# Blank gather slots of a graph kernel: one shared row of lowest values, or one row for each partition

## The reference

```python
def _L0_gnn_ref(X, adj):
    neg = jnp.finfo(X.dtype).min
    mask = adj != 0
    vals = jnp.max(jnp.where(mrows[:, :, None], X[None, :, :], neg), axis=1)
    has_nbr = jnp.any(mrows, axis=1)
    return jnp.where(has_nbr[:, None], vals, 0)
...
x = _layernorm(x + _L0_gnn_ref(x, adj), axis=-1)
x = _layernorm(x + _L1_gnn_ref(x, L1_gnn_W, L1_gnn_a, adj, 8192), axis=-1)
x = _layernorm(x + _L2_gnn_ref(adj, x, L2_gnn_W, L2_gnn_a), axis=-1)
x = _layernorm(x + _L3_gnn_ref(x, adj, L3_gnn_W, L3_gnn_a), axis=-1)
```

## Time and profile before

| what | value |
|---|---|
| median of 3 runs | 5,798.88 us |
| span of the profiled execution | 6,308.7 us |
| PE, DVE, ACT, POOL busy | 84%, 76%, 32%, 18% of the span |
| DMA queue q1 | 482.61 MB, 21.4% of 16 engines' span |
| DMA queue q0 | 73.21 MB, 11.5% |
| DMA queue q10 | 67.13 MB, 3.0% |
| mean granted TensorE clock | 0.922 |

### The profile page before, as it was taken

How to read it: one execution, slowest core, us unless ns; L and a number is a source line. 1 busy time by engine, 2 the same in 40 slices (tenths; PEclk the granted TensorE clock), 3 DMA queues, 4 the chain that set the end, 5 groups by cost and what they waited for, 6 DMA issues and landing times. The chain is left out here.

```text
span 6308.7 us, 93770 instructions
## 1 busy us (share of the span) xinstructions
PE 5282.6 (84%) x24260; PEld 2436.7 (39%) x24370; DVE 4783.5 (76%) x8750; ACT 2000.3 (32%) x2798; POOL 1155.2 (18%) x1367
## 2 busy tenths in 40 slices
PE   2766767666676654999999999979999998999999
PEld 1333333333333323333333333325444445444444
DVE  4676767677776664788888888887788886888887
ACT  1444444444444422555454545410000001000000
POOL 2545445444544530000000000000000000000000
PEclk8888888888888885999999999998999997999999
DMA  5777778777777722011111111001121211221210
GB/s 193 183 182 181 189 181 190 174 189 180 187 187 186 174 56 79 34 41 42 36 41 41 42 42 42 28 35 66 67 74 67 74 47 64 74 78 64 85 61 30
DMA packets 150569, 628.53 MB, mean 100 GB/s; under 512 B 30368, under 2 KB 39008, under 8 KB 92688
## 3 DMA queue, kind: packets, MB, share of 16 engines
q1 hardware_dynamic: 78464, 482.61, 21.4%
q0 software_dynamic: 34768, 73.21, 11.5%
q10 hardware_dynamic: 36864, 67.13, 3.0%
HBM read 551.49 MB, written 75.53 MB: 99 GB/s over the span
## 5 line engine op out<-in xcount | busy, mean ns | idle before, releaser
L1215 PE MATMUL bank<-w,GX 128*128 128x512 f32 x6144 | 2835.8, 607 | 31.7 <-DVE w L1442 22.6
L1215 PEld LDWEIGHTS bank<-w,GX 128*128 128x128 f32 x6144 | 1128.4, 191 | 1403.3 <-issue 1395.4
L1456 DVE SCALAR_TENSOR_TENSOR w<-q,E,m 128x512 f32<-128x512 f32 x2048 | 1449.1, 748 | 280.7 <-PE bank L1215 188.4
L283 POOL DMA_INDIRECT ring<-x_ext,idx x1051 | 1026.5, 977 | 1180.3 <-DVE X L519 354.8
L507 DVE TENSOR_TENSOR top<-top,sums 128x1024 f32<-128x1024 f32 x496 | 604.2, 1218 | 637.3 <-remote 379.1
L418 PE MATMUL sums<-lone,xs 128*128 128x512 fp8e4 x3072 | 857.7, 421 | 250.4 <-DVE top L507 136.5
L348 ACT ACTIVATE stage<-tp 128x1024 fp8e4<-128x1024 uint16 x512 | 523.5, 1024 | 1202.3 <-PE tp L390 573.4
L1442 DVE SCALAR_TENSOR_TENSOR w<-q,E,u 128x512 f32<-128x512 f32 x1024 | 762.4, 746 | 165.8 <-PE bank L1215 165.1
L1279 ACT ACTIVATE above<-bank,offset 128x512 fp8e4<-128x512 f32 x1024 | 649.1, 684 | 639.0 <-PE bank L1143 637.2
L1431 DVE SCALAR_TENSOR_TENSOR u<-theta,E,m 128x512 fp8e4<-128x512 f32 x1024 | 766.4, 750 | 95.2 <-issue 81.7
L418 PEld LDWEIGHTS sums<-lone,xs 128*128 128x128 bf16 x3072 | 300.5, 105 | 787.0 <-issue 568.6
(11 more groups left out here) (231 smaller groups left out, 3259.2 us busy)
## 6 DMA issues: line engine op xcount, KB each, us to landing
adjb<-in_adj SPq DMA_DIRECT2D x256, 1024.0 KB
m<-mask_t SPq DMA_DIRECT2D x192, 1024.0 KB, 4.9
mask_t<-stage ACTq DMA_DIRECT2D x256, 256.0 KB
ring<-x_ext,idx POOLq DMA_INDIRECT x1051
out<-X SPq DMA_DIRECT2D x16, 256.0 KB, 2.4
nhc<-nhd POOLq DMA_DIRECT2D x32, 2.0 KB, 1.7
Wn<-in_L_gnn_W SPq DMA_DIRECT2D x3, 64.0 KB
A<-in_L_gnn_a SPq DMA_DIRECT2D x6, 0.5 KB
```

The lines of the kernel that those rows point to most:

```text
L283: pool.indirect_dma_start(ring[:, s, :], None, x_ext, bass.IndirectOffsetOnAxis(ap=idx[:, k, s:s + 1], axis=0)).then_inc(done, 16)
L1215: last = nc.tensor.matmul(acc[b][:, :], GX[:, j, :], w[:, j % WR, :], start=(j == 0), stop=(j == T - 1))
L1456: nc.vector.scalar_tensor_tensor(out=w[:, j % WR, :], in0=q, scalar=E[:, j:j + 1], in1=m[:, b, j, :], op0=ALU.max, op1=ALU.mult).then_inc( ...
```

## The change

There are 128 rows of lowest values behind x instead of one. Partition p's blank slots get the number N + p. To that end `program` makes a constant `blank` of two columns, N + p and -127 - (N + p), which take the place of the two constants in L648 and L649. `top` is set on all 128 partitions, and its 128 pieces are written to `x_ext`. Nothing else is changed: the same slots are gathered, in the same order, by the same DMAs.

```diff
-            pool.dma_start(x_ext[N:N + 1, :], top[0:1, 0, 0:F]).then_inc(low_in, 16)
+            pool.dma_start(x_ext[N:N + P, :], top[:, 0, 0:F]).then_inc(low_in, 16)
...
-            nc.vector.memset(top[0:1, 0, 0:F], -BIG).then_inc(low_ready, 1)
+            nc.vector.memset(top[:, 0, 0:F], -BIG).then_inc(low_ready, 1)
...
-                    steps.do(nc.vector.scalar_tensor_tensor(out=pad[:, :], in0=base[:, :], scalar=-127.0 - N, in1=pad[:, :], op0=ALU.add, op1=ALU.mult))
-                    nc.vector.tensor_scalar(idx[:, (k + 1) % 2, :], pad[:, :], float(N), None, ALU.add).then_inc(idx_ready, 1)
+                    steps.do(nc.vector.scalar_tensor_tensor(out=pad[:, :], in0=base[:, :], scalar=blank[:, 0:1], in1=pad[:, :], op0=ALU.add, op1=ALU.mult))
+                    nc.vector.tensor_scalar(idx[:, (k + 1) % 2, :], pad[:, :], blank[:, 1:2], None, ALU.add).then_inc(idx_ready, 1)
...
-    x_ext = nc.dram_tensor("x_ext", [N + 1, F], F32, kind="Internal").ap()
+    x_ext = nc.dram_tensor("x_ext", [N + P, F], F32, kind="Internal").ap()
...
+            blank = sb0("blank", [P, 2], F32)
...
+                blank_i = c1.enter_context(nc.sbuf_tensor("blank_i", [P, 1], I32))
...
+                    s.do(nc.gpsimd.iota(blank_i[:, :], pattern=[[0, 1]], base=N, channel_multiplier=1))
                     s.do(nc.gpsimd.memset(sel[:, :, :], 0.0))
...
-                    dve.wait_ge(again, 4)
+                    dve.wait_ge(made, 16)
+                    nc.vector.tensor_copy(blank[:, 1:2], blank_i[:, :]).then_inc(again, 1)
+                    dve.wait_ge(again, 5)
+                    nc.vector.tensor_scalar(blank[:, 0:1], blank[:, 1:2], -1.0, -127.0, ALU.mult, ALU.add).then_inc(again, 1)
+                    dve.wait_ge(again, 6)
```

More of the change, by code:

```diff
@@ L146, in neighbour_max @@
 def neighbour_max(nc, x, adj, mask_t, x_ext, nm, deg, consts):
-    ident_b, ident, powers, code_no, firsts, found, due = consts
+    ident_b, ident, powers, code_no, firsts, blank, found, due = consts
     with ExitStack() as ctx:
@@ L1554, in _ @@
                     nc.vector.tensor_copy(firsts[:, :], firsts_f[:, :, :].rearrange("p w b -> p (w b)")).then_inc(again, 1)
-                    dve.wait_ge(again, 4)
-            neighbour_max(nc, x, adj, mask_t, x_ext, X, deg, (ident_b, ident, powers, code_no, firsts, has, rstd))
+                    dve.wait_ge(made, 16)
[3 more added lines that the diff above has]
+                    dve.wait_ge(again, 6)
+            neighbour_max(nc, x, adj, mask_t, x_ext, X, deg, (ident_b, ident, powers, code_no, firsts, blank, has, rstd))
             first_norm(nc, x, X, deg, has, stats)
```

## The result

The changed kernel takes 5,758.31 us, the median of 4 runs (5,751.61 to 5,773.01), against 5,804.8 for the kernel before (4 runs): ratio 0.991, 95% interval 0.989 to 0.9929, 46 us less. The profiled execution is one of the four, 5,751.61 us with a span of 5,750.0. The span of before that all rows above come from was 6,308.7. Most of that difference is not the change's, and it is not the profiler's either: the experiments show it.

The account below looks back on a forecast made before the run. The prediction took DMA occupancy to bound stage one, 26.0 us of a 26.5 us tile. A gain of 1.2 us in 64 tiles, 77 us, less 4 us of costs, gave 5,726 us from 5,799; range 5,640 to 5,825.

Parts of the forecast that it names:

- the three queues: Stage one: gathers, mask stores and adjacency loads take 11.1, 3.0 and 11.8 us of every DMA engine a tile, 26.0 together.
- the 4 us of costs: Index arithmetic and setup: 4 us added in sum, of which 3 us for the column operands in L648 and L649.
- That rival: Gathers: the change doesn't speed the packets, slow ones come from load, not one shared row; 5,803 us, chance 0.06.
- That is the ground of my forecast: Stage one, unprofiled runs: DMA needs 26.0 us of an estimated 26.5 to 28.8 us tile, so it is 90 to 98% occupied.
- DVE as the next bound: Stage one: once DMA falls to 18.5 us a tile, DVE's 24.1 us bounds it, a gain of 0 to 2.4 us.
- The half of 2.4 us: Stage one: half the possible gain taken because hand-offs never close fully, 1.2 us a tile, 77 us over 64 tiles.
- The columns: L648 and L649: a column operand replacing a constant costs 0 to 0.05 us each, 6 us at most, 3 taken.
- The issue gaps belong to profiling: Stage one: PE's issue idle, 5.1 us a tile, and the 510 us between profiled span and median come from profiling.
- The sign that the prediction gave for profiling: PE's issue idle gone in the profile and the median moving far less than the span would show gaps from profiling.
- That they aren't from the slow packets: Stage one, against the rival that PE's issue gaps are real and come from slow packets: 325 us, 5,474, chance 0.11.
- Nothing waits for DMA: Stage one: DMA at 98% may still meet every deadline, so only the 4 us of costs show; 5,803 us, chance 0.36.
- Slower: Gathers: 128 blank rows within 64 KB cost more than one row; at 30% dearer 5,953 us, chance 0.09.

Follow-up runs that it names:

- groups 2 and 3: Two sets of runs, each beside the kernel before on one chip: before took 5,809.1 us in the first and 5,810.7 us in the second.
- e2: Changed kernel with two blank rows, one for even and one for odd partitions: ratio 1.0029 to the kernel before, which took 6,271.4 us there.
- e10: Changed kernel plus three 1 MB copies a tile that nobody waits for until the stage ends: 5,757.3 us, ratio 0.9913 to the kernel before.
- e7: The kernel before, unchanged, as a run of its own for a profile: 5,812.7 us.
- e9: Changed kernel with all blank slots on one row again, the same kernel as e1, in another group: 5,816.1 us, ratio 1.0011 to the kernel before.
- e6: Changed kernel with blank rows ahead of x and a maximum with p instead of the columns: 5,747.5 us, ratio 0.9892 to the kernel before.
- groups 1 and 4: Two sets of runs, each beside the kernel before on one chip: before took 6,271.4 us in the first and 6,303.0 us in the second.
- e4: Changed kernel with sixteen blank rows, each shared by 8 neighbouring partitions: ratio 1.0033 to the kernel before, which took 6,271.4 us there.
- e1: Changed kernel with every partition's blank slots on the same one row: 6,301.0 us, ratio 1.0050 to the kernel before.
- e8: Changed kernel with two blank rows, the same kernel as e2, in another group: 5,757.9 us, ratio 0.991 to the kernel before.

## Why the prediction was right, and where not

- **The sign** holds, and the time lies in the range: 5,726 was forecast with its own range of 5,645 to 5,775, and 5,758 measured. Of the 73 us forecast, 46 came (51 and 53 in groups 2 and 3). The mechanism that gave the number did not hold, so that it came this near is in part luck. The sums of the prediction hold but for trifles: the three queues add up to 25.9 us, a gathered megabyte costs 3.6 times a stored one, and the range leaves out the 4 us of costs.
- **The packets**: 3.6 us a tile were forecast for q0, and 12.5% of 25.9 us is 3.2. The shares foretold for a 34.5 us tile (q0 about 11%, DMA near 0.55) came in e2, in the long condition: 11.0% and 0.56. L283 kept its duration (977 and 998 ns). The Trainium skill's rule, "DMA: Bandwidth & Descriptors", Latency and other measured facts, that an HBM access takes 0.2 us on average and 2 us at high load, doesn't explain the slow packets: e10 moves 369 GB/s with q0 at 0.18 us a packet. That rival falls.
- **"That is the ground of my forecast": DMA's 26.0 us a tile against 26.5.** The tile of the short condition was estimated well (1,400 / 53 = 26.4 us in e7, DMA share 0.93). Its DMA engines are busy 24.6 us of it, not 26.0. The step from there, that this occupancy holds the tile, failed in e10. Transfers that land late took its place (41.8 + 26.7 + 9.4 us of waits in e7), which the earlier trace rows seemed to exclude; they were read in a 34.5 us tile, 8 us longer, in which the waits that could name them came to 0.3 us each. DVE as the next bound was not refuted: it is busy 94% of the changed kernel's tile.
- **The half of 2.4 us.** It was a choice, 77 us; the rows measured 58, 0.9 us a tile. No run speaks for the half; a number near the right one had a wrong mechanism behind it.
- **The columns** were priced at 0 to 0.05 us each. They cost 0.06 (L648: 245 against 183 ns) and in L649 0.03 (301 against e7's 271; in e9, with one row like e7, 326). The 180 ns of the earlier trace rows were L649's in the long condition; the rest of the way to 301 is not the column's. In all the columns cost 5 us by e9, where 3 were taken. e6, which replaces them by another operation, saves 10 us, more than they cost.
- **"The issue gaps belong to profiling"** failed, and with it the use of the Trainium skill's "NOTIFIC — the notification-queue block", Interfaces, here: in groups 1 and 4 all 21 and 17 runs of before took over 6,250 us, and the profiled execution of e7 took 5,809.0 us, as its other runs did. So the 510 us are a condition in which whole groups run, not a cost of profiling. The sign that the prediction gave for profiling, PE's issue idle gone and the median moved far less than the span, did come, and would have been read wrongly. That they aren't from the slow packets was right (e2 to e4).
- **Nothing waits for DMA** (0.36) is nearly what happens in the long condition (7 to 13 us between e1 and e2 to e4); in the short one it fell. **Slower** (0.09) fell: 128 rows within 64 KB cost 0.19 us a packet, scattered ones 0.22.

## What to carry to other kernels

Don't let all partitions of an indirect DMA fall back on one row: two rows already cure it here, and rows reached by a maximum with p instead of per-partition column operands gave 5,747 us, the best of all versions. DMA engines that are busy 0.95 of the time aren't by themselves a bound; ask how long the packets hold an engine and which deadline lies behind them, and read those deadlines in a trace whose span is that of the runs. Where the profiled span and the median differ by 9%, get a second profile before explaining the gap.

## What the runs showed that was not expected

- 128 partitions on one 512 B row: 0.68 us a packet of 4 KB on average over all slots in e1; on two rows 0.23, on sixteen 0.22.
- Two conditions of stage one, 490 us apart (e1 ends it at 2,352.5 us, e9, the same kernel, at 1,862.0), with PE idle inside blocks of matmuls in the longer one. No run tells its cause.
- In the short condition 3 MB more of DMA traffic a tile, at 0.95 busy, cost nothing measurable (5,757.3 us against 5,757.9 of e8).
